# A ring of 24 heads for the cross attention's products, and gathers that read the table of slots itself, in a two-layer decoder kernel

## The chip, the cores and the metric

The kernel runs on one core of a Trainium2 chip. Its engines are TensorE (PE, with its weight loads shown as PEld), VectorE (DVE), ScalarE (ACT), GpSimd (POOL) and SyncE (SP, which only issues DMAs here); each has its own queue of instructions and runs it in order, and semaphores tie the queues together. The metric is the time of one execution on the device in microseconds, as the median of several runs.

## The reference, cut to what matters

The input is 64 sequences of 64 tokens with 256 channels, 4096 rows in all, that is 32 tiles of 128 rows. Six blocks follow one another, each with a layer norm ahead of it and a residual sum behind it: a linear attention, a recurrence over the context, a mixture of eight experts of which each token takes two, a banded attention, a cross attention and a gated feed-forward block with a small attention in it. The change lies in the stage that computes the last three. Its cross attention is unusual: for every token by itself, its 16 heads of the query look at the 16 heads of the context row at the same place.

```
Q = (q @ Wq.T + bq).reshape(bs, sl, H, HD)      # H = 16 heads of HD = 16
K = (k @ Wk.T + bk).reshape(bs, sl, H, HD)
V = (v @ Wv.T + bv).reshape(bs, sl, H, HD)
score = jnp.einsum('bshd,bsgd->bshg', Q, K)
weight = jax.nn.softmax(score, axis=-1)
attn = jnp.einsum('bshg,bsgd->bshd', weight, V).reshape(bs, sl, nf)
return attn @ Wo.T + bo
```

So a token has 16 x 16 scores, each a sum of 16 products, and then 256 outputs, each again a sum of 16 products. No weights are shared between tokens there, so this is not work for TensorE.

## The kernel before

The program has three stages: the linear attention (first, to about 1600 us), the recurrence with the experts (to about 2005 us), and `layer_one`, which computes the last three blocks and adds up the experts' outputs on its way. Only `layer_one` changes.

`layer_one` is a software pipeline over the 32 tiles. `FIRST` gives each piece of work a stage number (G = -2 gathers the experts' outputs, D and its helpers are the banded attention, En, E and Et the cross attention at 1, 2 and 3, F and Ft the attention of the last block, M and Md its feed-forward). `iterate` writes out one pass after another; in pass i a piece with stage number s works on tile i - s. Each engine has its own list of pieces, and the order of that list is the order of its instructions in every pass. Nothing is reordered by a scheduler.

POOL's list is: `power("F", 2)` (inverse roots for the last block's norm, written l_rsF), `products_av`, `power("D", 1)`, `power("E", 1)` (l_rsD and l_rsE), `products_qk`, `gather`. So in a pass POOL first makes the products of weights and values of tile t (16 instructions of 128x256, one for each head, L1740), then the products of queries and keys of tile t + 1 (16 more, L1733), then the gathers of a later tile.

Both kinds of product are written into one buffer, `prod`, of 16 heads (16 KB in each partition). DVE sums them up: four reductions of four heads each make the scores (`et_scores`, L2238), then `et_shift`, ACT's exponential (L2120) and `et_weights` (its last instruction is L2254, which counts the semaphore E_w up), and four more reductions make the attention's output (`et_values`, L2262, each of which counts E_att up). In DVE's list the four of a kind don't stand together: other pieces lie between them, and they come in the order of quarters 0, 2, 1, 3. `products_qk` of tile t waits until all four `et_values` of tile t - 1 have run, since it overwrites what they read:

```
wait_if(pool, S("E_att"), 4 * t)
...
for h in range(H):
    nc.gpsimd.tensor_tensor(out=prod[:, h], ...
```

`products_av` waits for E_w alone. `q`, the query, is one buffer, filled by ACT (L2016) once the products of the tile before are made; `kv`, the keys and values, is three buffers loaded by SP.

`gather` fetches the two experts' rows of each token with two indirect DMAs (L1752) which POOL itself describes. Their row numbers are first copied from the table `slots` (32 tiles x 2 numbers in each partition) into a small tile `of_tile` (L1747); a multiplication of constants into `ready` stands ahead of the copy and another behind it (L1746, L1750).

`fwo`, a weight of 256 x 256, has a buffer of its own; PE uses it once, at the very start of the stage, for a product with `fa` (woa).

Of the kernel before, what the change touches and what calls it, by code (L numbers as in the profile page):

```python
# [8 lines left out]
ALU = mybir.AluOpType  # L9
ACT = mybir.ActivationFunctionType  # L10

P = 128
SEQ = 64
SEQS = 64
D = 256
# [1527 lines left out]
def layer_one(nc, new_sem, x_sb, ident, slots, wts, outs, kvd, bias_rows, a):  # L1543
# [25 lines left out]
    AX = mybir.AxisListType.X  # L1569
    FIRST = dict(G=-2, Dn=-1, D=0, Dt=1, En=1, E=2, Et=3, F=4, Ft=5, M=7, Md=8)  # L1570
    with ExitStack() as ctx:
# [19 lines left out]
        fwqk, fwv, fwo = sb("fwqk", [P, DC, 4 * P]), sb("fwv", [P, DC, D]), sb("fwo", [P, DC, D])  # L1591
# [12 lines left out]
        of_tile, ready = sb("of_tile", [P, 2], mybir.dt.uint32), sb("ready", [P, 1])  # L1604
# [20 lines left out]
        prod = sb("prod", [P, H, H, HD])  # L1625
# [57 lines left out]
        def _(sp):  # L1683
# [3 lines left out]
            for tensor, name in ((fwo, "fwo"), (fa, "fa")):  # L1687
                sp.dma_start(tensor[:], a[name]).then_inc(S("wo_in"), 16)
# [22 lines left out]
        def _(pool):  # L1711
# [14 lines left out]
            def products_qk(t):  # L1726
                pool.wait_ge(S("E_q"), t + 1)
                pool.wait_ge(S(f"kv_in{t % 3}"), 16 * (t // 3 + 1))
                wait_if(pool, S("E_att"), 4 * t)
                qv = q[:].rearrange("p (h d) -> p h d", d=HD)  # L1730
                kk = kv[t % 3][:, 0, :].rearrange("p (g d) -> p g d", d=HD)
                for h in range(H):
                    nc.gpsimd.tensor_tensor(out=prod[:, h], in0=qv[:, h:h + 1, :].to_broadcast([P, H, HD]), in1=kk,  # L1733
                                            op=ALU.mult).then_inc(S("E_pqk"), 1)

            def products_av(t):
                pool.wait_ge(S("E_w"), t + 1)
                vv = kv[t % 3][:, 1, :].rearrange("p (d g) -> p d g", d=HD)
                for h in range(H):
                    nc.gpsimd.tensor_tensor(out=prod[:, h], in0=sco[:, h:h + 1, :].to_broadcast([P, HD, H]), in1=vv,  # L1740
                                            op=ALU.mult).then_inc(S("E_pav"), 1)

            def gather(t):
                wait_if(pool, S("G_ready"), 2 * t)
                wait_if(pool, S("G_x"), 2 * t)
                nc.gpsimd.tensor_tensor(out=ready[:], in0=neghalf[:, 0:1], in1=neghalf[:, 0:1], op=ALU.mult).then_inc(S("G_ready"), 1)  # L1746
                nc.gpsimd.tensor_copy(of_tile[:], slots[:, tile(t), :].rearrange("p t k -> p (t k)")).then_inc(S("G_at"), 1)  # L1747
                pool.wait_ge(S("G_ready"), 2 * t + 1)
                pool.wait_ge(S("G_at"), t + 1)
                nc.gpsimd.tensor_tensor(out=ready[:], in0=neghalf[:, 0:1], in1=neghalf[:, 0:1], op=ALU.mult).then_inc(S("G_ready"), 1)  # L1750
                for k in range(2):
                    nc.gpsimd.indirect_dma_start(got[k][:], None, outs[:, :],  # L1752
                                                 bass.IndirectOffsetOnAxis(ap=of_tile[:, k:k + 1], axis=0)).then_inc(S(f"G_in{k}"), 16)
# [394 lines left out]
        def _(dve):  # L2148
# [84 lines left out]
            def et_scores(k):  # L2233

                def piece(t):
                    wait_if(dve, S("E_pav"), H * t)
                    dve.wait_ge(S("E_pqk"), H * t + 4 * k + 4)
                    nc.vector.reduce_sum(sco[:, 4 * k:4 * k + 4, :], prod[:, 4 * k:4 * k + 4], axis=AX).then_inc(S("E_sc"), 1)  # L2238
                return piece
# [17 lines left out]
            def et_values(k):  # L2257

                def piece(t):
                    wait_if(dve, S("E_aTp"), t)  # L2260
                    dve.wait_ge(S("E_pav"), H * t + 4 * k + 4)
                    nc.vector.reduce_sum(att[:].rearrange("p (h d) -> p h d", d=HD)[:, 4 * k:4 * k + 4, :], prod[:, 4 * k:4 * k + 4],  # L2262
# [206 lines left out]
```

## Time and profile before

| | |
|---|---|
| three timed runs | 3121.44 us median, 3116.44 to 3129.29 |
| the profiled execution, from the first to the last instruction | 3137.3 us (its own time is not listed apart from this span) |
| the third stage in it | about 2005 to 3137 us |
| PE / DVE / ACT / POOL busy | 90% / 82% / 62% / 65% of the span |

The profiled execution is 15.9 us longer than the median. Starts in the rows are microseconds from its first instruction. A row of a timeline gives start, duration, engine, line, operation, what is written and read, the shapes, how many instructions are merged into the row, and in brackets how long the engine had been idle ahead of it and what ended that. A busy engine need not be one that others wait for; the list of waits tells this.

### The profile page before, as it was taken

What the parts mean: (1) busy time and instruction counts of PE and PEld (TensorE: products, weight loads), DVE (VectorE), ACT (ScalarE), POOL (GpSimd) and SP (SyncE); (2) the same over time, 40 slices, a digit from 0 to 9 for tenths busy, and PEclk for the clock granted to TensorE, in tenths of its full rate; (3) what the DMA queues carried; (4) which work ended last, traced back from release to release, by engine and by line L of the source; (5) the groups of instructions that cost most, each with busy time, mean ns of one, the idle gap of its engine ahead of it and who ended that gap; (6) DMA issues with size and microseconds to landing.
All of it is one profiled execution on the core that took longest, in us unless ns stands there. A gap on an engine that the chain in (4) does not pass through costs nothing. (4 is left out here: it accounts for less than half of the span.)

```text
span 3137.3 us, 68808 instructions
## 1 busy us (share of the span) xinstructions
PE 2826.3 (90%) x21864; PEld 2304.6 (73%) x21864; DVE 2581.5 (82%) x5745; ACT 1949.5 (62%) x4213; POOL 2038.0 (65%) x2535
## 2 busy tenths in 40 slices
PE   6999999999999999997786799657899999999978
PEld 3888888888888888886454577435777777777767
DVE  6888888888888888886597566478999999999973
ACT  5888877787877778785343333245565656565632
POOL 5886666666666666665487200178888888888870
PEclk8999999999999999998897899767999999999999
DMA  4564444444444444442422222300000000000000
GB/s 145 168 206 158 134 145 136 141 141 145 135 147 128 140 134 138 154 130 82 160 103 74 85 77 77 124 14 18 20 20 25 20 25 20 25 18 27 15 9 11
DMA packets 178643, 288.05 MB, mean 92 GB/s; under 512 B 42255, under 2 KB 103832, under 8 KB 177707
## 3 DMA queue, kind: packets, MB, share of 16 engines
q1 hardware_dynamic: 172206, 267.46, 25.8%
q0 software_dynamic: 6144, 16.79, 1.7%
q8 instruction: 171, 2.80, 0.3%
q14 instruction: 122, 1.00, 0.1%
HBM read 221.99 MB, written 53.78 MB: 88 GB/s over the span
## 5 line engine op out<-in xcount | busy, mean ns | idle before, releaser
L1740 POOL TENSOR_TENSOR l_prod<-l_sco,l_kv 128x256 f32<-128x256 f32 x512 | 380.0, 781 | 47.5 <-DVE l_sco L2254 47.5
L1733 POOL TENSOR_TENSOR l_prod<-l_q,l_kv 128x256 f32<-128x256 f32 x512 | 358.6, 740 | 62.1 <-DVE l_att L2262 62.1
L717 DVE SCALAR_TENSOR_TENSOR a_cq<-a_PQ,a_taps,a_cq 128x504 f32<-128x504 f32 (+2 forms) x384 | 281.7, 734 | 74.0 <-ACT a_cq L583 64.9
L717 DVE SCALAR_TENSOR_TENSOR a_ck<-a_PK,a_taps,a_ck 128x504 f32<-128x504 f32 (+2 forms) x384 | 280.6, 731 | 9.7 <-ACT a_ck L583 0.6
L341 POOL TENSOR_TENSOR a_tq<-a_cq,a_tq 128x512 f32<-128x512 f32 x128 | 165.5, 1293 | 131.3 <-ACT a_tq L589 131.2
L328 POOL TENSOR_TENSOR a_hrs<-a_hve,a_neghalf 128x8 f32<-128x8 f32 x128 | 209.4, 1636 | 25.9 <-DVE a_hve L734 25.4
L484 PE MATMUL a_Y<-a_wo,a_og_parts 128*128 128x256 f32 x1536 | 206.2, 284 | 4.2 <-POOL a_og_parts L335 4.2
L411 PEld LDWEIGHTS a_X<-a_wv,a_xb 128*128 128x128 f32 x1536 | 199.9, 188 | 12.1 <-issue 1.2
L411 PE MATMUL a_PQ<-a_x_hi,a_wqk 128*128 (+1 forms) x512 | 195.3, 422 | 12.0 <-issue 11.3
L341 POOL TENSOR_TENSOR a_tk<-a_ck,a_tk 128x512 f32<-128x512 f32 x128 | 163.3, 1276 | 64.1 <-ACT a_tk L589 64.1
L411 PE MATMUL a_X<-a_wv,a_xb 128*128 128x256 f32 x1536 | 204.2, 282 | 0.8 <-DMA a_xb<-a_x_lo 0.8
L484 PEld LDWEIGHTS a_Y<-a_wo,a_og_parts 128*128 128x128 f32 x1536 | 195.1, 192 | 5.5 <-issue 5.4
L602 ACT ACTIVATE a_hk<-a_PK,a_lncol 128x512 f32<-128x512 f32 x128 | 99.9, 781 | 154.5 <-PE a_PK L503 154.5
L596 ACT ACTIVATE a_nq<-a_TQ,a_hnb,a_hrs 128x128 f32<-128x128 f32 x512 | 191.6, 460 | 1.5 <-POOL a_hnb L331 1.0
L596 ACT ACTIVATE a_nk<-a_TK,a_hnb,a_hrs 128x128 f32<-128x128 f32 x512 | 191.1, 457 | 0.0
L411 PE MATMUL a_X<-a_x_hi,a_wg 128*128 (+1 forms) x512 | 184.3, 400 | 2.3 <-DVE a_og L742 2.3
L411 PE MATMUL a_PK<-a_x_hi,a_wqk 128*128 (+1 forms) x512 | 182.6, 397 | 0.0
L335 POOL TENSOR_TENSOR a_og_parts<-a_og,a_og_parts 128x512 fp32r<-128x512 f32 x128 | 166.1, 1298 | 19.9 <-ACT a_og_parts L609 19.9
L1712 POOL MEMSET l_cmask<- 128x512 bf16 x1 | 0.5, 524 | 255.4 <-POOLq L2354 255.4
L583 ACT ACTIVATE a_cq<-a_PQ,a_taps 128x512 f32<-128x512 f32 x128 | 99.8, 779 | 101.3 <-PE a_PQ L411 101.3
L771 DVE TENSOR_TENSOR_SCAN a_em<-a_dr,a_dm 128x256 f32<-128x256 f32 x128 | 159.7, 1247 | 0.0
L2262 DVE TENSOR_REDUCE l_att<-l_prod 128x64 f32<-128x1024 f32 x128 | 151.7, 1206 | 8.6 <-POOL l_prod L1740 8.3
(403 smaller groups left out, 8534.5 us busy)
## 6 DMA issues: line engine op xcount, KB each, us to landing
a_wqk<-qk_parts SPq DMA_DIRECT2D x112, 512.0 KB, 3.3
a_wv<-v_parts SPq DMA_DIRECT2D x56, 512.0 KB, 3.7
a_wg<-g_parts SPq DMA_DIRECT2D x112, 256.0 KB, 3.1
a_wo<-o_parts SPq DMA_DIRECT2D x112, 256.0 KB, 2.8
a_dr<-decays SPq DMA_DIRECT2D x256, 64.0 KB, 2.6
m_hs<-sorted_rows SPq DMA_DIRECT2D x72, 128.0 KB, 2.0
sorted_outs<-m_ys SPq DMA_DIRECT2D x72, 128.0 KB, 1.7
qk_parts<-a_wqk SPq DMA_DIRECT2D x16, 512.0 KB, 3.3
```

Source lines behind the costliest of these rows:

```text
L328: nc.gpsimd.tensor_tensor(out=hrs[q][:], in0=hve[q][:], in1=neghalf[:], op=ALU.pow).then_inc(s_hrstd, 1)
L335: nc.gpsimd.tensor_tensor(out=og_parts[q][:, 1, :], in0=og[q][:], in1=og_parts[q][:, 0, :].bitcast(F32), op=ALU.subtract).then_inc(og_lo, 1)
L341: nc.gpsimd.tensor_tensor(out=t[i][p][:], in0=c[i][p][:], in1=t[i][p][:], op=ALU.mult).then_inc(s_silu, 1)
L411: last = nc.tensor.matmul(out, lhs(i, k), rhs(j, k), start=at_pass == PASSES[0], stop=at_pass == PASSES[-1])
L484: last = nc.tensor.matmul(Y[:, j, :], og_parts[p][:, i, j * P:(j + 1) * P], wo[p][:, w, :], start=first and j % 2 == 0 and k == 0, stop=Tr ...
L596: nc.scalar.activation(nrm[i][q][:, j, :], TB[i][:, j, :], ACT.Identity, bias=hnb[q][:, k:k + 1], scale=hrs[q][:, k:k + 1]).then_inc(s_nor ...
L602: nc.scalar.activation(hat[i][q][:], PB[i][:], ACT.Identity, bias=lncol[:, 2 * i + 1:2 * i + 2], scale=lncol[:, 2 * i:2 * i + 1]).then_inc ...
L717: nc.vector.scalar_tensor_tensor(out=acc, in0=src, scalar=taps[p][:, tap + k:tap + k + 1], in1=acc, op0=ALU.mult, op1=ALU.add).then_inc(s_ ...
L771: nc.vector.tensor_tensor_scan(out=flat(em[q]), data0=flat(dr[q]), data1=flat(dm[q]), initial=0.0, op0=ALU.mult, op1=ALU.add).then_inc(s_e ...
L1733: nc.gpsimd.tensor_tensor(out=prod[:, h], in0=qv[:, h:h + 1, :].to_broadcast([P, H, HD]), in1=kk, op=ALU.mult).then_inc(S("E_pqk"), 1)
L1740: nc.gpsimd.tensor_tensor(out=prod[:, h], in0=sco[:, h:h + 1, :].to_broadcast([P, HD, H]), in1=vv, op=ALU.mult).then_inc(S("E_pav"), 1)
L2262: nc.vector.reduce_sum(att[:].rearrange("p (h d) -> p h d", d=HD)[:, 4 * k:4 * k + 4, :], prod[:, 4 * k:4 * k + 4], axis=AX).then_inc(S("E ...
```

## The change

`prod` becomes a ring of 24 heads. The products of tile t take 32 places in a row from place 32t on, modulo 24: the first 16 for queries and keys, the next 16 for weights and values. The first eight heads of `products_qk` of a tile then fall on places that nothing reads any more; heads 8 to 15 fall on the places of heads 0 to 7 of the tile before's weights and values, which the reductions of quarters 0 and 1 read. Since DVE's order is 0, 2, 1, 3, the wait now stands ahead of head 8 and asks for three reductions instead of four. The wait for the fourth moves to `products_av`. The reductions take their quarter at the same places.

The ring has 8 KB more in each partition. `fwo` loses its buffer (2 KB) and becomes a view of the ring's first two heads; it is loaded and used before the ring is. `gather` loses its copy, its two multiplications and their two semaphores, and the indirect DMA reads its row numbers from `slots`.

```diff
+    RING = 24
-        fwqk, fwv, fwo = sb("fwqk", [P, DC, 4 * P]), sb("fwv", [P, DC, D]), sb("fwo", [P, DC, D])
+        fwqk, fwv = sb("fwqk", [P, DC, 4 * P]), sb("fwv", [P, DC, D])
-        of_tile, ready = sb("of_tile", [P, 2], mybir.dt.uint32), sb("ready", [P, 1])
-        prod = sb("prod", [P, H, H, HD])
+        prod = sb("prod", [P, RING, H, HD])
+        fwo = prod[:, 0:2].rearrange("p h g d -> p h (g d)")
...
             def products_qk(t):
                 pool.wait_ge(S("E_q"), t + 1)
                 pool.wait_ge(S(f"kv_in{t % 3}"), 16 * (t // 3 + 1))
-                wait_if(pool, S("E_att"), 4 * t)
...
                 for h in range(H):
-                    nc.gpsimd.tensor_tensor(out=prod[:, h], in0=qv[:, h:h + 1, :].to_broadcast([P, H, HD]), in1=kk,
+                    if h == H // 2 and t:
+                        pool.wait_ge(S("E_att"), 4 * t - 1)
+                    nc.gpsimd.tensor_tensor(out=prod[:, (2 * H * t + h) % RING], in0=qv[:, h:h + 1, :].to_broadcast([P, H, HD]), in1=kk,
...
             def products_av(t):
                 pool.wait_ge(S("E_w"), t + 1)
+                wait_if(pool, S("E_att"), 4 * t)
...
-                    nc.gpsimd.tensor_tensor(out=prod[:, h], in0=sco[:, h:h + 1, :].to_broadcast([P, HD, H]), in1=vv,
+                    nc.gpsimd.tensor_tensor(out=prod[:, (2 * H * t + H + h) % RING], in0=sco[:, h:h + 1, :].to_broadcast([P, HD, H]), in1=vv,
...
             def gather(t):
-                wait_if(pool, S("G_ready"), 2 * t)
                 wait_if(pool, S("G_x"), 2 * t)
-                nc.gpsimd.tensor_tensor(out=ready[:], in0=neghalf[:, 0:1], in1=neghalf[:, 0:1], op=ALU.mult).then_inc(S("G_ready"), 1)
-                nc.gpsimd.tensor_copy(of_tile[:], slots[:, tile(t), :].rearrange("p t k -> p (t k)")).then_inc(S("G_at"), 1)
-                pool.wait_ge(S("G_ready"), 2 * t + 1)
-                pool.wait_ge(S("G_at"), t + 1)
-                nc.gpsimd.tensor_tensor(out=ready[:], in0=neghalf[:, 0:1], in1=neghalf[:, 0:1], op=ALU.mult).then_inc(S("G_ready"), 1)
                 for k in range(2):
                     nc.gpsimd.indirect_dma_start(got[k][:], None, outs[:, :],
-                                                 bass.IndirectOffsetOnAxis(ap=of_tile[:, k:k + 1], axis=0)).then_inc(S(f"G_in{k}"), 16)
+                                                 bass.IndirectOffsetOnAxis(ap=slots[:, t, k:k + 1], axis=0)).then_inc(S(f"G_in{k}"), 16)
...
             def et_scores(k):
...
-                    nc.vector.reduce_sum(sco[:, 4 * k:4 * k + 4, :], prod[:, 4 * k:4 * k + 4], axis=AX).then_inc(S("E_sc"), 1)
+                    at = (2 * H * t + 4 * k) % RING
+                    nc.vector.reduce_sum(sco[:, 4 * k:4 * k + 4, :], prod[:, at:at + 4], axis=AX).then_inc(S("E_sc"), 1)
```

`et_values` changes in the same way, with `at = (2 * H * t + H + 4 * k) % RING`.

The next fences show POOL's queue. In brackets stand the semaphores that an instruction waits for, under the names that their numbers had in the first stage: in the queue before, a_zset is E_w, a_zdec is E_att, a_zdecay is E_q, a_x_ld4 is the load of `kv`, a_xhi, a_zmm and a_nb_set are the statistics of D, E and F, and a_xrstd, a_xvar and a_xnorm are those of `gather`; in the changed queue, which has two fewer, a_zdecay is E_w, a_zdec is E_att, a_zmm is E_q, a_xT, a_xhi and a_zT are the statistics of D, E and F, and a_xvar is `gather`'s.

One pass in the middle of the stage on POOL, before: the products of weights and values, two powers, the products of queries and keys, the gather, a power.

```order
L1740 TENSOR_TENSOR l_prod<-l_sco,l_kv 128x256 [waits a_zset]
L1740 TENSOR_TENSOR l_prod<-l_sco,l_kv 128x256 x15
L1723 TENSOR_TENSOR l_rsD<-l_veD,l_neghalf 128x1 [waits a_xhi]
L1723 TENSOR_TENSOR l_rsE<-l_veE,l_neghalf 128x1 [waits a_zmm]
L1733 TENSOR_TENSOR l_prod<-l_q,l_kv 128x256 [waits a_zdec,a_x_ld4,a_zdecay]
L1733 TENSOR_TENSOR l_prod<-l_q,l_kv 128x256 x15
L1746 TENSOR_TENSOR l_ready<-l_neghalf 128x1 [waits a_xrstd,a_xvar]
L1747 COPY l_of_tile<-slots 128x2
L1750 TENSOR_TENSOR l_ready<-l_neghalf 128x1 [waits a_xnorm,a_xvar]
L1752 DMA l_got<-sorted_outs,l_of_tile 128x256 x2
L1723 TENSOR_TENSOR l_rsF<-l_veF,l_neghalf 128x2 [waits a_nb_set]
```

The same pass on POOL now:

```order
L1743 TENSOR_TENSOR l_prod<-l_sco,l_kv 128x256 [waits a_zdec,a_zdecay]
L1743 TENSOR_TENSOR l_prod<-l_sco,l_kv 128x256 x15
L1724 TENSOR_TENSOR l_rsD<-l_veD,l_neghalf 128x1 [waits a_xT]
L1724 TENSOR_TENSOR l_rsE<-l_veE,l_neghalf 128x1 [waits a_xhi]
L1735 TENSOR_TENSOR l_prod<-l_q,l_kv 128x256 [waits a_x_ld4,a_zmm]
L1735 TENSOR_TENSOR l_prod<-l_q,l_kv 128x256 x7
L1735 TENSOR_TENSOR l_prod<-l_q,l_kv 128x256 [waits a_zdec]
L1735 TENSOR_TENSOR l_prod<-l_q,l_kv 128x256 x7
L1749 DMA l_got<-sorted_outs,slots 128x256 [waits a_xvar]
L1749 DMA l_got<-sorted_outs,slots 128x256
L1724 TENSOR_TENSOR l_rsF<-l_veF,l_neghalf 128x2 [waits a_zT]
```

No instruction has changed its place in the queue; the wait for E_att has moved from the first product of queries and keys to the ninth, a second one stands at the first product of weights and values, and three small instructions ahead of the gathers are gone.

The start of the stage on POOL, before: the mask is made, then the first gather is set up.

```order
L1717 AFFINE_SELECT l_cmask<-l_cmask 64x512
L1746 TENSOR_TENSOR l_ready<-l_neghalf 128x1 [waits a_xstat]
L1747 COPY l_of_tile<-slots 128x2
L1750 TENSOR_TENSOR l_ready<-l_neghalf 128x1 [waits a_xnorm,a_xvar]
L1752 DMA l_got<-sorted_outs,l_of_tile 128x256 x2
```

The start of the stage on POOL now:

```order
L1718 AFFINE_SELECT l_cmask<-l_cmask 64x512
L1749 DMA l_got<-sorted_outs,slots 128x256 [waits a_xstat]
L1749 DMA l_got<-sorted_outs,slots 128x256
L1724 TENSOR_TENSOR l_rsD<-l_veD,l_neghalf 128x1 [waits a_xT]
L1749 DMA l_got<-sorted_outs,slots 128x256 [waits a_xvar]
```

The first gather stands right behind the mask (a_xstat counts the mask's instructions).

The end of the stage on POOL, before: the products of the last two tiles, with no power of D or E between them any more.

```order
L1740 TENSOR_TENSOR l_prod<-l_sco,l_kv 128x256 [waits a_zset]
L1740 TENSOR_TENSOR l_prod<-l_sco,l_kv 128x256 x15
L1733 TENSOR_TENSOR l_prod<-l_q,l_kv 128x256 [waits a_zdec,a_x_ld5,a_zdecay]
L1733 TENSOR_TENSOR l_prod<-l_q,l_kv 128x256 x15
L1723 TENSOR_TENSOR l_rsF<-l_veF,l_neghalf 128x2 [waits a_nb_set]
L1740 TENSOR_TENSOR l_prod<-l_sco,l_kv 128x256 [waits a_zset]
L1740 TENSOR_TENSOR l_prod<-l_sco,l_kv 128x256 x15
```

The end of the stage on POOL now:

```order
L1743 TENSOR_TENSOR l_prod<-l_sco,l_kv 128x256 [waits a_zdec,a_zdecay]
L1743 TENSOR_TENSOR l_prod<-l_sco,l_kv 128x256 x15
L1735 TENSOR_TENSOR l_prod<-l_q,l_kv 128x256 [waits a_x_ld5,a_zmm]
L1735 TENSOR_TENSOR l_prod<-l_q,l_kv 128x256 x7
L1735 TENSOR_TENSOR l_prod<-l_q,l_kv 128x256 [waits a_zdec]
L1735 TENSOR_TENSOR l_prod<-l_q,l_kv 128x256 x7
L1724 TENSOR_TENSOR l_rsF<-l_veF,l_neghalf 128x2 [waits a_zT]
```

Between the products of weights and values and the first eight of the next tile no wait for DVE is left.

## Rows read from the trace of the kernel before

**Rows 1.** The page: busy us, share of the span and instructions of each engine.
```profile
PE 2826.3 (90%) x21864; PEld 2304.6 (73%) x21864; DVE 2581.5 (82%) x5745; ACT 1949.5 (62%) x4213; POOL 2038.0 (65%) x2535
```

**Rows 2.** Windows, 24 whole passes: us, then busy of each engine, clock, DMA.
```profile
2189.21:2943.81 754.60, 686.75 (x5978) 552.71 (x5979) 718.57 (x1415) 449.33 (x1131) 656.52 (x960) 0.98 0.07 22
```

**Rows 3.** Waits, 2200 to 3000: engine, line, released by; total us, times, longest.
```profile
POOL l_prod L1733 <- DVE l_att L2262: 52.3, 25, 3.3
...
DVE l_att L2262 <- POOL l_prod L1740: 1.6, 1, 1.6
```

**Rows 4.** Timeline of POOL, one pass: start, us, line, instructions, idle ahead.
```profile
2488.50 12.00 POOL L1740 TENSOR_TENSOR l_prod<-l_sco,l_kv 128x256 f32<-128x256 f32 x16 [0.80 <-DVE l_sco L2254]
...
2500.96 0.54 POOL L1723 TENSOR_TENSOR l_rsE<-l_veE,l_neghalf 128x1 f32<-128x1 f32 x1
2503.44 11.08 POOL L1733 TENSOR_TENSOR l_prod<-l_q,l_kv 128x256 f32<-128x256 f32 x16 [1.95 <-DVE l_att L2262]
...
2515.60 1.06 POOL L1752 DMA_INDIRECT l_got<-sorted_outs,l_of_tile  x1 [0.46 <-issue]
...
2517.94 0.74 POOL L1723 TENSOR_TENSOR l_rsF<-l_veF,l_neghalf 128x2 f32<-128x2 f32 x1
2519.47 12.01 POOL L1740 TENSOR_TENSOR l_prod<-l_sco,l_kv 128x256 f32<-128x256 f32 x16 [0.80 <-DVE l_sco L2254]
```

**Rows 5.** Timeline of DVE in that pass, and one row of the next.
```profile
2499.63 2.33 DVE L2262 TENSOR_REDUCE l_att<-l_prod 128x64 f32<-128x1024 f32 x2
...
2504.44 0.44 DVE L2204 SCALAR_TENSOR_TENSOR l_hmD<-l_hmD,l_sink 128x16 f32<-128x16 f32 x1
...
2506.92 0.81 DVE L2279 TENSOR_TENSOR l_gm<-l_gmT,l_gm 16x128 fp32r<-16x128 f32 x1
...
2510.80 0.32 DVE L2209 TENSOR_SCALAR l_hmF<-l_hmF 128x16 f32<-128x16 f32 x1
...
2513.25 3.46 DVE L2238 TENSOR_REDUCE l_sco<-l_prod 128x64 f32<-128x1024 f32 x3
...
2542.25 0.79 DVE L2209 TENSOR_SCALAR l_hmF<-l_hmF 128x16 f32<-128x16 f32 x1
```

**Rows 6.** Timelines of POOL and DVE at the start of the stage.
```profile
2007.04 0.19 POOL L1746 TENSOR_TENSOR l_ready<-l_neghalf 128x1 f32<-128x1 f32 x1
...
2008.23 1.02 POOL L1752 DMA_INDIRECT l_got<-sorted_outs,l_of_tile  x1 [0.52 <-issue]
...
2015.18 0.48 DVE L2157 SCALAR_TENSOR_TENSOR x_sb<-l_got,wts,x_sb 128x256 f32<-128x256 f32 x1 [1.19 <-DMA l_got<-sorted_outs,l_of_tile]
...
2032.38 0.17 DVE L2204 SCALAR_TENSOR_TENSOR l_hmD<-l_hmD,l_sink 128x16 f32<-128x16 f32 x1
```

**Rows 7.** Timelines of POOL and DVE in the second and third pass with products.
```profile
2092.27 16.03 POOL L1733 TENSOR_TENSOR l_prod<-l_q,l_kv 128x256 f32<-128x256 f32 x16 [0.37 <-DVE l_att L2262]
...
2125.80 10.91 POOL L1733 TENSOR_TENSOR l_prod<-l_q,l_kv 128x256 f32<-128x256 f32 x16 [0.49 <-DVE l_att L2262]
...
2133.65 3.11 DVE L2209 TENSOR_SCALAR l_hmF<-l_hmF 128x16 f32<-128x16 f32 x1
```

**Rows 8.** Timelines of POOL and DVE in the last passes with products.
```profile
3004.88 11.02 POOL L1733 TENSOR_TENSOR l_prod<-l_q,l_kv 128x256 f32<-128x256 f32 x16 [2.02 <-DVE l_att L2262]
...
3019.85 10.98 POOL L1740 TENSOR_TENSOR l_prod<-l_sco,l_kv 128x256 f32<-128x256 f32 x16 [3.31 <-DVE l_sco L2254]
3036.24 11.02 POOL L1733 TENSOR_TENSOR l_prod<-l_q,l_kv 128x256 f32<-128x256 f32 x16 [5.41 <-DVE l_att L2262]
...
3015.99 1.22 DVE L2238 TENSOR_REDUCE l_sco<-l_prod 128x64 f32<-128x1024 f32 x1 [0.38 <-POOL l_prod L1733]
...
3027.94 3.17 DVE L2284 TENSOR_TENSOR l_x<-l_x2f,l_x 128x256 fp32r<-128x256 f32 x1
...
3044.65 2.35 DVE L2238 TENSOR_REDUCE l_sco<-l_prod 128x64 f32<-128x1024 f32 x2 [0.63 <-POOL l_prod L1733]
...
3047.36 1.22 DVE L2238 TENSOR_REDUCE l_sco<-l_prod 128x64 f32<-128x1024 f32 x1 [0.36 <-POOL l_prod L1733]
```

More of the change, by code:

```diff
@@ L1686, in _ @@
                 sp.dma_start(tensor[:], a[name]).then_inc(S("d_in"), 16)
-            for tensor, name in ((fwo, "fwo"), (fa, "fa")):
-                sp.dma_start(tensor[:], a[name]).then_inc(S("wo_in"), 16)
+            for tensor, name in ((fwo, "fwo"), (fa[:], "fa")):
+                sp.dma_start(tensor, a[name]).then_inc(S("wo_in"), 16)
             sp.dma_start(raw_in, a["win"]).then_inc(S("raw_in"), 16)
@@ L2261, in piece @@
                     dve.wait_ge(S("E_pav"), H * t + 4 * k + 4)
-                    nc.vector.reduce_sum(att[:].rearrange("p (h d) -> p h d", d=HD)[:, 4 * k:4 * k + 4, :], prod[:, 4 * k:4 * k + 4],
+                    at = (2 * H * t + H + 4 * k) % RING
+                    nc.vector.reduce_sum(att[:].rearrange("p (h d) -> p h d", d=HD)[:, 4 * k:4 * k + 4, :], prod[:, at:at + 4],
                                          axis=AX).then_inc(S("E_att"), 1)
```

## The prediction

> **What bounds the kernel now.** I read the page first [rows 1]: over the whole span DVE and PE are the busiest, POOL is at 65%. That mixes stages, so the next view is a window over 24 whole passes of the third stage, from the start of one tile's products of queries and keys to that of a tile 24 later [rows 2]: 754.60 us, 31.44 a pass. DVE is busy for 718.57 (95%), PE for 686.75 (91%), POOL for 656.52 (87%). The third view decides, the list of waits [rows 3]: POOL waited 52.3 us for DVE's reductions L2262 in 25 passes, about 2.1 each; this is the wait that the change takes away. The other way round DVE waited for POOL's products 1.6 us in 800. So in the middle of the stage POOL stands off the path: it is late only because DVE makes it late, and DVE doesn't notice.
>
> The timelines of one pass show the same in order [rows 4, 5]. POOL's products of weights and values run from 2488.50 to 2500.50 and the two powers to about 2501.5. Then it idles 1.95 us for the fourth reduction of quarters, makes the products of queries and keys to 2514.52, gathers, makes a power, and idles again (0.80) for DVE's softmax, which ends at 2519.4. DVE reads the last three quarters of those products from 2513.25 without a wait.
>
> **The change part by part.** The sum is made on the profiled execution, whose span is 15.9 us above the median; the difference is then taken off the median, 3121.44.
>
> *Middle of the stage, waits.* Now the products of queries and keys can start when the power l_rsE is done, at 2500.96 + 0.54, about 2501.5 [rows 4], 1.95 earlier. The ninth head is due 8 x 0.69 = 5.5 later, at 2507.0 (11.08 / 16 = 0.69 for one); the third reduction that it now waits for ended at 2499.63 + 2.33 = 2501.96 [rows 5]. So that wait costs nothing, and the fourth, at the products of weights and values, comes 16 us after its reduction (which ended just ahead of 2503.44). Behind it the gather saves its three small instructions: the first two starts in rows 6 are 2008.23 - 2007.04 = 1.19 apart, and with the idle time of 0.46 that still stands ahead of a DMA [rows 4] 0.7 is left. POOL then stands ready for the next products about 1.95 + 0.7 earlier, at 2516.1, and waits for the softmax at 2519.4 as before. Its start doesn't move, for DVE sets it. What is late next is DVE itself. Worth: 0.
>
> *Middle, the shared work of DVE and POOL.* Some small DVE instructions are longer beside POOL's products. L2204 takes 0.17 where POOL is idle [rows 6] and 0.44 one us into the products of queries and keys [rows 5]; 27 such rows read 0.43 to 0.45. It waits for the end of POOL's instruction: 1.00 / 0.69 = 1.45 instructions have gone, 0.38 us remain, 0.27 is seen. After the change the products start 1.95 earlier and L2204 comes 2.95 into them: 4.3 have gone, 0.5 us remains, so it should wait 0.34, or 0.07 more. The instructions behind it (L2279, L2209) keep their distances from it and so their waits. 27 x 0.07 = +1.9 us. Bounds: no wait, 27 x -0.27 = -7; a whole instruction's, 27 x (0.69 - 0.27) = +11. No other DVE instruction of two inputs in SBUF stands in the stretch that POOL newly fills (2501.5 to 2503.4) or newly leaves.
>
> *Start of the stage.* The first gather stands behind the mask and DVE waits 1.19 us for its rows [rows 6]. It is issued 0.7 earlier. Landing takes 5.9 us (2009.25 to 2015.18) beside the loads of all weights, so the rows may land when those let them: between 0 and -0.7; I take -0.4. Later gathers are needed a pass or more after they land.
>
> *First passes.* Tile 1's products wait 0.37 and tile 2's 0.49 [rows 7]. Here DVE does wait for POOL, so both come off the path: -0.85. In tile 2's pass L2209 took 3.11 us, to the moment when POOL's row of 16 products ended; that end also moves by 0.85. If it should not be held so this time, another 2 us go: from -0.85 to -3.
>
> *Last passes.* From 2944 on DVE has less to do. Tile 30's products wait 2.02, but DVE then waits for their end 0.38 only [rows 8]: -0.38. Tile 31's wait 5.41. They would start behind the products before, at 3019.85 + 10.98 - 0.38 = 3030.5, and end at 3041.5. DVE's last three score reductions then start when DVE is free, at 3044.65 - 0.63 - 0.38 = 3043.64, and take 3.46 as in rows 5, to 3047.10, where before they ended at 3047.36 + 1.22 = 3048.58: -1.48 with the 0.38 in it. So of 5.41 us only 1.1 is gained; DVE's other pieces cover the rest. From there one chain (softmax, last products, output, last tile's attention and feed-forward) leads to the end, so -1.5 stays. L2284 was held to the end of POOL's row here [rows 8], and now the next row follows without a pause; held on to its ninth head, at 3036, it would delay all this by 5 us and leave a loss of some 4. That is the upper bound, -1.5 the value, since the gap between the rows stays an instruction's.
>
> `fwo` as a view and the four extra places move nothing: the ring is first written when tile 0 has a query, and that comes behind `fwo`'s product in PE's queue. At nothing too are the reads from `slots`: the gather's own 1.06 and 0.95 us stay, and even doubled they would lie in POOL's idle 3.3 us.
>
> Sum: 0 + 1.9 - 0.4 - 0.85 - 1.5 = -0.85 us, so 3121.44 - 0.85 = 3120.6.
>
> **The rivals.** *DVE held to the end of POOL's row (slower).* Two DVE instructions were held not for one product but until the row of 16 was over: L2209 from 2133.65 to 2136.76, when POOL's row ended at 2136.71 [rows 7], and L2284 from 3027.94 to 3031.11, when POOL's row ended at 3030.83 [rows 8]. In the middle L2209 stands 7.36 into POOL's row and takes 0.32, in some passes 0.79 [rows 5]. Now it stands 9.3 into it with 1.8 to go. If every pass held it, 27 x (1.8 - 0.2) = +43 us, 3164; if L2204 were held until the new wait ahead of the ninth head, 5.5 - 2.95 - 0.27 = 2.3, 27 times, +62, 3183. It decides as soon as the hold happens in the repeating passes, since those are alike to 0.02 us. Against it: both cases lie in passes at the ends of the stage where pieces are still or already missing from DVE's list; in the middle L2279 comes between POOL's products 3 us ahead of L2209, before and after. Chance 0.08.
> The Trainium skill (SBUF — State Buffer, "Who interferes with whom") says that a DVE instruction with two SBUF inputs, and a GpSimd instruction that reads SBUF, take a shared pair of ports in turns, and that the loser is blocked for the whole of the other's instruction. By that rule a hold ends with one product, so the price would be at most the +11 above, about 3130; the rows with 3.11 and 3.17 go beyond it.
>
> *The passes even out (faster).* The pass in rows 4 lasts 30.97 (2488.50 to 2519.47), the mean is 31.44 [rows 2]; in some of the longer ones L2209 takes 0.79 [rows 5]. If POOL's new phase spared DVE that, 24 x 0.47 = -11.3 more, 3109. Against it: L2209's wait hangs on its distance to L2279, which doesn't change. Chance 0.12.
>
> *POOL sets the pace after all (faster).* Then 2.1 + 0.7 come off each of 27 passes: -76 us, 3046. DVE's 1.6 us of waits speak against it [rows 3]. Chance 0.03.
>
> *The change doesn't do what it says.* The products start where they did, held by E_q or the power instead. Against it: the row of the wait names the reduction as what came last, not E_q [rows 4], and l_rsE is done by 2501.5. Then the time is that of before, 3121, or up to 1 less for the gather. Chance 0.07.
>
> **How the numbers follow.** The forecast, DVE sets the pace, gets 0.70: 3120.6, with a range of its own from -7 - 0.7 - 3 - 1.5 = -12 to 11 - 0.85 + 4 = +14, 3109 to 3135, all within 0.5% (15.6 us, about what a measurement of this kernel can tell from no change); the three runs of before already spread over 13 us. Left out of the range are the held instruction (0.08), POOL's pace (0.03) and a few per cent of drift, so 3108 to 3135. Faster by over 0.5%: POOL's pace 0.03 and a sixth of the 0.12, where evening out and lower bounds add up past 15.6, and 0.05 for a gain that I don't see: 0.10. Slower: the held instruction 0.08 and 0.02 for the like: 0.10. Within 0.5%: 0.80.
>
> **What would show it.** Right, if POOL's wait for L2262 is gone in the list of waits and its wait for L2254 has grown from 0.8 to about 3.3 us a pass; if L2204 reads about 0.5 and L2209 0.3 or 0.8; if DVE stays at 95% in the middle; if tile 31's products start about 5.7 earlier and the last score reductions end 1.5 earlier. Wrong, if DVE's share falls or a pass is under 30.9 us (then POOL did set the pace), or if L2204, L2209 or L2284 read over 1 us in pass after pass.

## The result, and the profile after

The changed kernel takes 3288.98 us (median of four runs, 3253.97 to 3308.55); the kernel before, run beside it, took 3125.36. The ratio is 1.0474 (95% interval 1.0438 to 1.0509): 4.7% slower, outside the predicted range. This ratio leaves out the longest of the four, 3308.55, as a slow run; that is the one profiled, and the holds that its trace shows stand alike in a run that isn't slow (the one with one input, below). The profiled span is 3306.3 us, 169.0 above that of before. In the changed kernel L1735 are the products of queries and keys (before: L1733), L1743 those of weights and values (L1740), L2201 is the small DVE instruction that the prediction calls L2204, L2252 ends the softmax (L2254).

First the page: busy us, share of the span and instructions of each engine, then three groups (busy, mean ns of one, idle time ahead and its releaser).

```profile
PE 2849.2 (86%) x21864; PEld 2308.6 (70%) x21864; DVE 2740.3 (83%) x5745; ACT 1946.4 (59%) x4213; POOL 2010.1 (61%) x2439
...
L1743 POOL TENSOR_TENSOR l_prod<-l_sco,l_kv 128x256 f32<-128x256 f32 x512 | 380.7, 782 | 164.6 <-DVE l_sco L2252 164.6
L1735 POOL TENSOR_TENSOR l_prod<-l_q,l_kv 128x256 f32<-128x256 f32 x512 | 349.4, 722 | 0.0
L2201 DVE SCALAR_TENSOR_TENSOR l_hmD<-l_hmD,l_sink 128x16 f32<-128x16 f32 x32 | 213.7, 6677 | 1.1
```

The last of these groups in the kernel before:

```profile
L2204 DVE SCALAR_TENSOR_TENSOR l_hmD<-l_hmD,l_sink 128x16 f32<-128x16 f32 x32 | 13.6, 424 | 1.1
```

Beside [rows 1] DVE has 158.8 us more to do with the same 5745 instructions. One group of 32 has 200.1 us more: L2201, 16 elements in each partition, is busy for 6.7 us on average. Other small instructions of DVE have become shorter, which gives back the difference. POOL's wait ahead of the products of queries and keys, 52.3 us in [rows 3], is gone, as intended. The same 24 passes as in [rows 2], from tile 4's products to tile 28's (us, busy of PE, PEld, DVE, ACT and POOL, clock, DMA):

```profile
2200.80:3104.06 903.26, 713.42 (x5969) 560.45 (x5970) 848.67 (x1413) 445.87 (x1129) 638.08 (x889) 0.89 0.06 18
```

They take 903.26 us instead of 754.60. Of the 24, 21 last 38.52 on average and three 31.46; before, the mean was 31.44. So 21 x 7.08 = 148.7 us of the 169.0 lie here, and all in the 21. DVE is busy for 130.1 us of these (848.67 - 718.57); for the other 18.6 it waits longer than before. PE is busy 26.7 us longer at a mean granted clock of 0.89 (0.98 before), but for 79% of the time instead of 91%, and the waits below show it waiting for DVE. The rest, added up from the starts of the products, lies at the two ends of the stage: +18.7 in the first four passes, +8.8 behind tile 28's, and -7.2 ahead of the first products, whose start lies anywhere from 2054.53 to 2074.75 in the runs below.

What a long pass looks like: POOL and DVE, from 2412 on (start, us, instruction, idle ahead).

```profile
2424.63 0.53 POOL L1724 TENSOR_TENSOR l_rsE<-l_veE,l_neghalf 128x1 f32<-128x1 f32 x1
2425.14 10.89 POOL L1735 TENSOR_TENSOR l_prod<-l_q,l_kv 128x256 f32<-128x256 f32 x16
2436.20 1.04 POOL L1749 DMA_INDIRECT l_got<-sorted_outs,slots  x1 [0.17 <-issue]
...
2444.53 0.72 POOL L1724 TENSOR_TENSOR l_rsF<-l_veF,l_neghalf 128x2 f32<-128x2 f32 x1 [6.04 <-DVE l_veF L2173]
2450.58 12.02 POOL L1743 TENSOR_TENSOR l_prod<-l_sco,l_kv 128x256 f32<-128x256 f32 x16 [5.33 <-DVE l_sco L2252]
```

```profile
2425.75 1.20 DVE L2261 TENSOR_REDUCE l_att<-l_prod 128x64 f32<-128x1024 f32 x1
2426.88 1.20 DVE L2198 TENSOR_REDUCE l_hmD<-l_SS 128x16 f32<-128x1024 f32 x1
2428.11 7.95 DVE L2201 SCALAR_TENSOR_TENSOR l_hmD<-l_hmD,l_sink 128x16 f32<-128x16 f32 x1
2436.09 0.18 DVE L2204 TENSOR_TENSOR l_hmD<-l_sink,l_hmD 128x16 f32<-128x16 f32 x1
2436.38 1.23 DVE L2209 SCALAR_TENSOR_TENSOR l_exD<-l_SS,l_hmD 128x1024 f32<-128x1024 f32 x1
2437.63 0.28 DVE L2278 TENSOR_TENSOR l_gm<-l_gmT,l_gm 16x128 fp32r<-16x128 f32 x1
```

L2201 starts 2.97 us into POOL's row and ends at 2436.06; POOL's sixteenth product ends at 2436.03. Its successor of the same size takes 0.18. An instruction that stands like this until the row is over is called held from here on. In three of the 24 passes L2201 isn't held, in two of them at the same distance; here it stands 2620.72 - 2617.75 = 2.97 into the row (POOL, where the view ends within the row, then DVE):

```profile
2617.75 7.61 POOL L1735 TENSOR_TENSOR l_prod<-l_q,l_kv 128x256 f32<-128x256 f32 x11
```
```profile
2620.72 0.52 DVE L2201 SCALAR_TENSOR_TENSOR l_hmD<-l_hmD,l_sink 128x16 f32<-128x16 f32 x1
```

The other engines wait for what follows the held instruction. The list of waits from 2200 to 3105 (engine, released by; total us, times, longest):

```profile
PE l_SS L1794 <- DVE l_exD L2209: 148.2, 22, 8.8
ACT l_exD L2018 <- DVE l_exD L2209: 129.8, 22, 7.9
POOL l_rsF L1724 <- DVE l_veF L2173: 127.3, 21, 6.1
POOL l_prod L1743 <- DVE l_sco L2252: 126.7, 24, 5.8
```

The last and the first of them in the kernel before, from 2190 to 2944:

```profile
POOL l_prod L1740 <- DVE l_sco L2254: 26.0, 24, 1.8
...
PE l_SS L1797 <- DVE l_exD L2212: 1.7, 2, 1.1
```

### The profile page after: what moved, and what is told of

Read it like the earlier page. It is cut to its first block and busy times, and to the rows that moved or that the text cites. A ratio compares the mean times of both kernels' runs of the same rounds, so it can differ in the third digit from the quotient of the medians.

```text
span 3306.3 us, 68680 instructions
## 1 busy us (share of the span) xinstructions
PE 2849.2 (86%) x21864; PEld 2308.6 (70%) x21864; DVE 2740.3 (83%) x5745; ACT 1946.4 (59%) x4213; POOL 2010.1 (61%) x2439
## 5 line engine op out<-in xcount | busy, mean ns | idle before, releaser
L1743 POOL TENSOR_TENSOR l_prod<-l_sco,l_kv 128x256 f32<-128x256 f32 x512 | 380.7, 782 | 164.6 <-DVE l_sco L2252 164.6
L1735 POOL TENSOR_TENSOR l_prod<-l_q,l_kv 128x256 f32<-128x256 f32 x512 | 349.4, 722 | 0.0
L341 POOL TENSOR_TENSOR a_tq<-a_cq,a_tq 128x512 f32<-128x512 f32 x128 | 165.5, 1293 | 130.1 <-ACT a_tq L589 130.0
L2201 DVE SCALAR_TENSOR_TENSOR l_hmD<-l_hmD,l_sink 128x16 f32<-128x16 f32 x32 | 213.7, 6677 | 1.1
L1794 PE MATMUL l_SS<-l_cmask,l_identb 128*128 128x512 bf16 x64 | 29.9, 565 | 178.9 <-DVE l_exD L2209 178.9
L2261 DVE TENSOR_REDUCE l_att<-l_prod 128x64 f32<-128x1024 f32 x128 | 151.7, 1206 | 8.9 <-POOL l_prod L1743 8.6
```

Source lines behind the costliest of these rows:

```text
L341: nc.gpsimd.tensor_tensor(out=t[i][p][:], in0=c[i][p][:], in1=t[i][p][:], op=ALU.mult).then_inc(s_silu, 1)
L1735: nc.gpsimd.tensor_tensor(out=prod[:, (2 * H * t + h) % RING], in0=qv[:, h:h + 1, :].to_broadcast([P, H, HD]), in1=kk, op=ALU.mult).then_i ...
L1743: nc.gpsimd.tensor_tensor(out=prod[:, (2 * H * t + H + h) % RING], in0=sco[:, h:h + 1, :].to_broadcast([P, HD, H]), in1=vv, op=ALU.mult).t ...
L2201: nc.vector.scalar_tensor_tensor(out=hm[k][:, 1, :], in0=hm[k][:, 0, :], scalar=SC, in1=sink[:], op0=ALU.mult, op1=ALU.add).then_inc(S("D_ ...
```

## The experiments

Line numbers move by a few with each edit; the small instruction is the one that writes l_hmD from l_hmD and l_sink. The 24 passes are always those from tile 4's products of queries and keys to tile 28's. Each ratio is taken beside the kernel before in the same session (medians of 3131.51, 3130.85 and 3129.29 us in the three).

**What in the change does it?** The theory: the wait that was moved. Rivals: the ring's places, or the gathers.

*The wait back in its place*, ring and gathers as changed:

```diff
+                wait_if(pool, S("E_att"), 4 * t)
...
                 for h in range(H):
-                    if h == H // 2 and t:
-                        pool.wait_ge(S("E_att"), 4 * t - 1)
```

> The ring of 24 and the gathers from the table of slots stay; the wait for all four reductions stands ahead of the first product of queries and keys again. Theory (the 160 us are L2201 on DVE, held to the end of POOL's row of products because the row now starts 1.95 us earlier): the row starts 1.0 us ahead of that instruction as before, it takes 0.44 us in every pass, and the time is that of the kernel before, 3121 within 10. Rival (the place of the ring in SBUF, or reading row numbers from the table, costs the time): the time stays at 3250 to 3310.

Measured 3131.35 us, ratio 1.0004 (0.9990 to 1.0017). The small instruction stands 1.00 into the row again and takes 0.43 to 0.45 in all 24 passes:

```profile
2563.76 0.44 DVE L2200 SCALAR_TENSOR_TENSOR l_hmD<-l_hmD,l_sink 128x16 f32<-128x16 f32 x1
```

*The gathers alone* in the kernel before (the diff's `gather` and nothing else):

> The kernel before with only the gathers changed to read from the table of slots. Theory: no hold, POOL's products still start behind the fourth reduction; the first gather lands up to 0.7 us earlier, so 3118 to 3125. Rival (the gather's earlier descriptors or its reads from the table disturb DVE): slower by over 15 us.

Measured 3131.39, ratio 1.0003 (0.9983 to 1.0022). So neither the places in the ring nor the gathers cost anything that can be measured; the loss comes from the moved wait, by which POOL now starts its row right behind the row before.

**What is the hold?** *The row pushed against DVE* by a memory set of POOL (into a spare buffer, `gap`) ahead of it, a little longer in each pass:

```diff
+                if t >= 3:
+                    nc.gpsimd.memset(gap[:, 0:27 * (t - 2)], 0.0)
```

> The changed kernel with one memset of a spare buffer on POOL ahead of the first product of queries and keys of tiles 3 to 31, 27 elements long for tile 3 and 27 more for each further tile, so that the row starts between 0 and about 0.8 us later in steps of some 0.03 us. It is a map of one run: at which distance from the start of POOL's row is L2201 held. Theory A (what counts is the point within one POOL instruction of 0.68 us at which DVE asks): held and not held change over within the 0.8 us and come back after 0.68. Theory B (what counts is how far into the row DVE asks, beyond the first one or two products): held throughout, 2.1 to 3.0 us into the row. Theory C (chance, since at 2.97 us both occur): held and not held mixed at every distance.

One run, 3251.4 us. The distance into the row went from 2.88 down to 2.38 in the 24 passes, with three off the line (1.74, 3.00 and 3.16). Held were the seven passes from 2.84 to 2.71 without exception, and one at 3.00; the one at 2.88 was not, and below 2.71 both kinds mix, at the very same distance too. Two neighbours, 2.56 and 2.56 into their rows (which start at 2710.49 and 2749.34):

```profile
2713.05 8.35 DVE L2204 SCALAR_TENSOR_TENSOR l_hmD<-l_hmD,l_sink 128x16 f32<-128x16 f32 x1
...
2751.90 0.26 DVE L2204 SCALAR_TENSOR_TENSOR l_hmD<-l_hmD,l_sink 128x16 f32<-128x16 f32 x1
```

13 of 24 passes were held, always until the row ended. Where the instruction isn't held, it takes 0.22 to 0.60 (once 0.80), that is, at most about one product (0.68) more than the 0.17 with POOL idle. This is nearest to theory C: there are two outcomes, a wait of one product or of the whole rest of the row, and the distance in hundredths of a microsecond doesn't settle which.

*A pause of POOL ahead of each product of queries and keys*, by a wait for its own product before (the expectations call this a drained row):

```diff
                     if h == H // 2 and t:
                         pool.wait_ge(S("E_att"), 4 * t - 1)
+                    if h:
+                        pool.wait_ge(S("E_pqk"), H * t + h)
```

> The changed kernel, but each product of queries and keys waits for the one before it (on the semaphore that POOL counts itself), so that POOL's row has a gap behind each product. Theory (DVE is held because POOL's products follow each other without a gap): no hold over one product, L2201 under 0.8 us in every pass, row about 12 to 13 us instead of 10.9, and the time 3110 to 3130. Rival (something other than the gapless row makes L2201 slow): L2201 still takes 8 us and the time stays at 3250 to 3310.

Measured 3113.40, ratio 0.9936 (0.9913 to 0.9958): no hold in any row with pauses, and faster than both kernels. The instruction is at the same 2.97 and takes hardly longer than with POOL idle ([rows 6], 0.17); POOL's row has become 2 us longer:

```profile
2409.54 0.19 DVE L2203 SCALAR_TENSOR_TENSOR l_hmD<-l_hmD,l_sink 128x16 f32<-128x16 f32 x1
```
```profile
2406.57 12.95 POOL L1737 TENSOR_TENSOR l_prod<-l_q,l_kv 128x256 f32<-128x256 f32 x16
...
2423.86 12.01 POOL L1745 TENSOR_TENSOR l_prod<-l_sco,l_kv 128x256 f32<-128x256 f32 x16 [1.16 <-DVE l_sco L2254]
```

*One pause only*, ahead of the ninth product. The moved wait stands there too, but it is satisfied before POOL comes to it:

```diff
+                    if h == H // 2:
+                        pool.wait_ge(S("E_pqk"), H * t + h)
```

> The changed kernel, but ahead of the ninth product of queries and keys POOL waits also for its own eighth product, so that the row has one real gap in its middle. The disputed DVE instruction (D's shift, the two-input one) still starts about 2.97 us into the row, where seven products stand without a gap behind it to the ninth head at 5.5. Theory 'a gap ends the hold': it reads 2.5 to 2.9 us in most passes instead of 7.95, and the time is 3289 - 25 x 5.2 = about 3160. Rival 'who is held is held to the last product of the row': it still reads about 8 and the time is about 3289. Rival 'the hold needs the whole row of 16 ahead of it': it reads under 0.6 and the time is 3115 to 3131.

3168.78 in one run, beside 3130.85 for the kernel before. Held instructions now end at the pause, 5.5 us into the row; 15 of 24 passes hold one:

```profile
2392.93 0.51 DVE L2203 SCALAR_TENSOR_TENSOR l_hmD<-l_hmD,l_sink 128x16 f32<-128x16 f32 x1
2424.13 2.57 DVE L2203 SCALAR_TENSOR_TENSOR l_hmD<-l_hmD,l_sink 128x16 f32<-128x16 f32 x1
```

So a pause ends a hold. A wait for something that has long happened does not: in the changed kernel, with the moved wait alone at the ninth product, the instruction stood 7.95 us, past it.

*Three pauses*, ahead of the products 2, 5 and 8 (counted from 0):

```diff
+                    if h in (2, 5, 8):
+                        pool.wait_ge(S("E_pqk"), H * t + h)
```

> The changed kernel with an own wait of POOL ahead of the products 2, 5 and 8 of queries and keys alone, so three gaps instead of fifteen. The disputed instruction comes at 2.97 + 0.1 us, the sixth product stands at about 3.7. Theory 'a hold lasts to the next gap': it reads 0.5 to 0.8 in every pass, no pass is held, POOL's row is about 11.4 us long, and passes are about 30.5 us: 3112 to 3125, ratio 0.995 to 0.999. Rival 'one gap may be lost again': in a part of the passes it reads 2.7 (the second gap passed over), 3130 to 3170.

3118.97, ratio 0.9969 (0.9956 to 0.9983); the instruction reads 0.42 to 0.74 in all 24 passes, none is held, and a pass takes 30.80.

**Which instructions can be held?** *One input instead of two*: D's shift computed as F's is, which leaves out L2201 and its successor.

```diff
-                    if k == "D":
-                        nc.vector.scalar_tensor_tensor(out=hm[k][:, 1, :], in0=hm[k][:, 0, :], scalar=SC, in1=sink[:], op0=ALU.mult,
...
-                        nc.vector.tensor_tensor(out=hm[k][:, 2, :], in0=sink[:], in1=hm[k][:, 1, :], op=ALU.subtract).then_inc(S("D_shift"), 1)
...
+                    nc.vector.tensor_scalar(hm[k][:, 2, :], hm[k][:, 0, :], -SC, None, ALU.mult).then_inc(S(k + "_shift"), 1)
```

> The changed kernel, but D's shift is made as F's is, by one DVE instruction of one input (the maximum times a constant); the instruction with two inputs in SBUF, which was held, and its successor are left out. The value is the same but for rounding. Rows, ring and waits stay. Theory 'it is held because of its two inputs in SBUF': the new instruction at 2.97 reads 0.17 to 0.6 and the time is 3289 - 25 x 7.0 = about 3115. Rival 'any DVE instruction from SBUF to SBUF that starts in the row may lose so': it reads 7.9 in most passes and the time is 3280 to 3290. Rival 'the hold moves to the next such instruction' (the difference of the two parts of the modulation, about 2 us behind it): that one reads up to 5.5 and the time is about 3220 to 3250.

3293.99, ratio 1.0516 (1.0490 to 1.0543): the first rival, a little above its range. An instruction with one input from SBUF is held just the same, in 21 of 24 passes:

```profile
2427.80 7.94 DVE L2200 TENSOR_SCALAR l_hmD<-l_hmD 128x16 f32<-128x16 f32 x1
```

*No shift at all*: DVE subtracts the maximum from the scores, which it reads from PSUM, and ACT's exponential takes the factor. L2201, L2204 and L2206 fall away.

```diff
...
+                    nc.vector.tensor_tensor(out=ex[k][:], in0=ss, in1=hm[k][:, 0, :].unsqueeze(2).to_broadcast([P, H, SEQ]),
+                                            op=ALU.subtract).then_inc(S(k + "_arg"), 1)
...
-                    nc.scalar.activation(ex[k][:], ex[k][:], ACT.Exp).then_inc(S(k + "_exp"), 1)
+                    nc.scalar.activation(ex[k][:], ex[k][:], ACT.Exp, scale=SC).then_inc(S(k + "_exp"), 1)
```

> The changed kernel without the disputed instruction and its two kindred (the shifts of D and F): DVE subtracts the maximum from the scores directly (scores from PSUM), and ACT's exponential takes the factor. Rows of products, ring and waits stay as in the changed kernel, with no gaps. Theory 'the loss sits in that one instruction, and the ring by itself is worth what the passes without a hold show' (31.05 us a pass in the changed kernel and 30.51 in the run with one gap, beside 31.44 before): two dependent instructions with 0.5 + 0.6 us fall away from each pass for D and 0.3 for F: about 30 us a pass, 3090 to 3115, a ratio of 0.985 to 0.995. Rival 'the hold moves to the next instruction from SBUF to SBUF in the same row' (the difference of the modulation's two parts, then some 4 us into the row): it reads up to 7 us in a part of the passes, 3150 to 3300.

3241.19, ratio 1.0369 (1.0339 to 1.0399): the rival again. The subtraction from PSUM takes 1.22 at 3.04 into the row, but the next instruction with both inputs in SBUF, 4.3 us into it in most passes, is held in 19 of 24 passes (35.77 us each; the other five take 29.92):

```profile
2747.90 0.64 DVE L2270 TENSOR_TENSOR l_gm<-l_gmT,l_gm 16x128 fp32r<-16x128 f32 x1
2778.05 6.75 DVE L2270 TENSOR_TENSOR l_gm<-l_gmT,l_gm 16x128 fp32r<-16x128 f32 x1
```

The prediction cited the Trainium skill (SBUF — State Buffer, "Who interferes with whom"), by which the loser waits for one instruction. The same section names tensor_scalar among the operations that can take the shared ports, and says that tensor_reduce never contends; L2200 above agrees with the first, and L2261, a reduction of products in SBUF that takes 1.20 us within POOL's row, with the second. On the length the measurement decides: 7.95 us is 7.95 / (10.89 / 16) = 11.7 products, not one.

**Is the ring worth anything?** *The pauses in the kernel before*, its waits and its one buffer kept:

```diff
+                    if h:
+                        pool.wait_ge(S("E_pqk"), H * t + h)
                     nc.gpsimd.tensor_tensor(out=prod[:, h], ...
```

> The kernel before, with only the own wait of POOL ahead of each product of queries and keys (no ring, no new gather). It tells what the 0.64% of the drained ring was. Theory 'the gain is the drain's, the ring gives nothing': DVE's small instructions lose their 0.27 and 0.6 us waits in each pass, ratio 0.993 to 0.996, about 3111. Rival 'the drain needs the slack that the ring gave POOL': its row is 1.9 us longer, POOL had 0.80 + 0.46 us of idle time behind it, so it ends about 0.7 us late for the softmax or the reductions in each pass: 3121 - 20 + 19 = within 0.2% of before, 3115 to 3128.

3190.10, ratio 1.0186 (1.0172 to 1.0201), worse than either expectation. POOL still waits 2 to 3 us for DVE, its row is 1.8 us longer (12.88), the products of weights and values follow without idle time, and now others wait for POOL (waits from 2300 to 2940):

```profile
POOL l_prod L1735 <- DVE l_att L2264: 50.2, 19, 3.2
...
ACT l_nmF L2000 <- POOL l_rsF L1723: 31.5, 20, 2.0
...
DVE l_sco L2240 <- POOL l_prod L1735: 11.1, 23, 0.9
```

A pass takes 33.14; two of the 24, of 39.10 and 39.28 us, also have a hold like those of the next run, the others take 32.58. So here the pauses pay only with the slack that the moved wait and the shorter gather give POOL (1.16 us left in the run with pauses, above).

*The shifts left out of the kernel before*, with the same edit:

> The kernel before, with only the shifts left out as in the run without the shifts (no ring, old gather). It parts the ring's share of a gain from the shifts' share. Theory 'the ring is worth 0.4 to 0.9 us a pass once nothing is held': this kernel gains 27 x (0.44 + 0.3 + 0.3) = about 28 us, ratio 0.990 to 0.994, and the ring with the same edit is 10 to 20 us better. Rival 'the ring is worth nothing in any case': both are alike within 0.2%.

3121.69, ratio 0.9982 (0.9968 to 0.9996), a smaller gain than the theory's. In two of its passes, without any ring, a DVE instruction of `d_rope`, a piece of the banded attention, is held through the other row of POOL (weights and values; 2200.35 to 2211.31):

```profile
2201.99 9.61 DVE L2190 TENSOR_TENSOR l_qkt<-l_qr,l_rt 128x256 f32<-128x256 f32 x1
```
```profile
2200.35 10.96 POOL L1740 TENSOR_TENSOR l_prod<-l_sco,l_kv 128x256 f32<-128x256 f32 x16
```

The two passes with it last 37.84 and 37.34, the other 22 take 30.50 on average, 0.94 less than the 31.44 of before. So two holds take back 14.2 us of what the edit gains, and the ring itself is not what makes a hold possible. POOL's row of 16 is 10.96 us here, where it is 12.0 beside a DVE that isn't held.

*Ring, pauses and no shifts together:*

> As the run without the shifts, and POOL also waits for its own product ahead of each product of queries and keys. Theory: what was lost to holds and single waits in that row is gone already, the drain adds 1.9 us to POOL's row, which POOL's slack covers (26.3 us of waits for the softmax in 21 passes of the drained ring, 1.25 each) only as long as DVE's pass is not shorter than POOL's 12.0 + 12.95 + 4.5 = 29.5 us and the order of their waits; 3095 to 3112. Rival: POOL becomes the bound as in the old kernel with the drain: 3120 or more.

3098.34, ratio 0.9906 (0.9888 to 0.9925): the best version, 0.9% faster than the kernel before and 5.8% than the changed one. None of the 24 passes has a hold, and one takes 30.10. That is 23.35 us ahead of the kernel just above; by the traces 14.2 of them are its two holds, and 24 x (30.50 - 30.10) = 9.6 is what the ring, the gather and the pauses add in passes without a hold. What the ring gives alone, with neither holds nor pauses, no run shows.

*Pauses in both rows*, the shifts kept:

> The changed kernel with an own wait of POOL ahead of each product in both rows (queries and keys as in the run with drained rows, and weights and values too). Theory 'what is gained there comes from DVE's instructions that no longer wait for POOL': the second row is about 0.125 x 15 = 1.9 us longer, POOL still has slack (it waited 51.5 us for the softmax in the run with one drained row, about 1.6 a pass), DVE's instructions beside the second row get shorter by some tenths, but POOL's pass grows to just about DVE's: within 0.3% of the kernel with one drained row, 3104 to 3122. Rival 'POOL becomes the bound': 0.3 to 0.8 us more a pass, 3122 to 3137.

3141.76, ratio 1.0028 (1.0011 to 1.0045): slower than with one row of pauses, 3113.40. POOL's second row grows from 12.0 to 13.2 us, DVE starts to wait for products (10.1 us in 18 waits from 2300 to 2940), and a pass takes 31.52. That POOL comes to bound it, the rival, fits; it ended a little above that rival's range.

## Why the prediction was wrong

- *Middle, waits: right.* POOL's idle time for the reductions is 0.0 instead of 52.3 us, and its wait for the softmax grew instead. In the three passes without a hold that costs nothing: 31.46 beside 31.44.
- *Middle, the shared work of DVE and POOL: the step that failed.* The term for L2204 was 27 x 0.07 = 1.9 us with +11 as its upper bound. The place was right: 2.95 into the row was forecast, 2.96 to 3.00 measured in 20 of the 21 held passes. The size was not: a wait of 0.34 was forecast, and the instruction took 7.94 to 7.96 in those 20 (9.01 in the 21st, at 1.92), which makes a held pass 7.08 us longer. The term and its bound took it that an instruction waits for one product of POOL at most. The rows with 3.11 and 3.17 [rows 7, 8] already showed the other outcome; the prediction saw it and kept it out of the range, as a rival with a small chance. Its own sign of being wrong, L2204 over 1 us in pass after pass, is what came.
- *The rival "DVE held to the end of POOL's row"* was the right mechanism at the right instruction, with a chance of 0.08 and a price of 2.3 us a pass instead of 7.1. Both the price and the argument behind the chance were wrong. The price took the satisfied wait ahead of the ninth product as a pause; the run with one real pause there is what gave 2.57. The argument against it, that the two holds lay in passes at the ends of the stage where DVE's list is incomplete, was a coincidence taken for a cause: with the list complete L2201 is held in the middle, and so, for 9.6 and 9.2 us, is an instruction of `d_rope` in the kernel before with its shifts left out or pauses put in. Why the middle of the kernel before has no hold stays as open as what decides between the two outcomes. That a hold repeats, since the passes are alike, came true 21 times of 24.
- *L2279 and L2209 keep their distances and so their waits: wrong, at little cost.* Behind a hold they run with POOL's row over: 0.28 and 0.17 instead of 0.81 and 0.32 to 0.79. With L2201's successor (0.18 instead of 0.65) that takes at least 1.1 us off the 7.95 - 0.44 = 7.51 of the hold. A held pass is still 7.08 longer, since DVE then waits for the scores of F that PE makes late (21.8 us from 2200 to 3105; 1.6 in the 24 passes before).
- *Start, gathers, `fwo`: right as far as can be measured.* DVE's wait for the first rows fell from 1.19 us to nothing, yet the gathers alone give 1.0003.
- *First passes:* whether the 0.85 was gained isn't shown, since holds bury it; all four rows from tile 1's products to tile 4's have one, of 9.55, 9.39, 8.18 and 9.01 us.
- *Last passes: right in direction, too small.* Tile 31's products start 31.36 + 2.02 - 27.72 = 5.66 us earlier (5.7 forecast). From the fourth reduction ahead of tile 30's products to the end it is 3137.3 - 3003.51 = 133.79 us before and 3306.3 - 3179.39 = 126.91 after, -6.9 instead of -1.5. Of the other 5.4, 5.1 fit the two holds of L2284 at the end, 3.17 [rows 8] and a second of 3.49, which read 0.68 and 0.86 now; the upper bound of +4 had the first longer. That is luck: one such hold is there again in the run with the gathers alone (2.95), three in the one with the wait back (up to 5.45).

## What to carry to other kernels

A row of GpSimd instructions that follow each other without a pause can hold a small VectorE instruction until it is over. Giving an off-path engine its idle time back moves its rows against the other engines' instructions, and here that was enough. Where a trace shows even one or two such holds, price the whole rest of the row in every repeating pass, and don't take it for unlikely because it has been rare so far. Pauses of 0.13 us (a wait for the engine's own last result) in the row capped the price here, where that engine had slack for them.

## What the runs showed of the hardware

- An instruction of 16 elements a partition on DVE stood for up to 9.6 us beside POOL's products; in the changed kernel it ends 0.03 to 0.04 us behind the row's last product, in the run with one pause at that pause. Such a pause cost (12.95 - 11.06) / 15 = 0.13 us of POOL's time, 11.06 being the row of a pass without a hold.
- A wait that was already satisfied when POOL arrived did not end a hold (7.95 us from 2.97 on, past the ninth product at 5.5).
- POOL's row is shorter while DVE is held: 10.96 instead of 12.0 us for the products of weights and values (the run with the shifts left out of the kernel before), 10.88 to 10.91 instead of 10.98 to 11.07 for those of queries and keys (the 24 passes of the changed kernel). So in passes without a hold POOL loses time beside DVE too.
- Held were instructions with two inputs in SBUF and some of a single input (7.94 in the run with one input; L2209 in [rows 7]); the reductions and the subtraction from PSUM that stand in the same rows read 1.20 to 1.23 throughout.
- What decides between a wait of one product and of the whole row stays open. At one and the same distance (2.56 us) one pass was held and another not. Other distances were never held: in the kernel before L2204 at 1.00 and L2279 at 3.47 took 0.43 to 0.45 and 0.79 to 0.81 in all 24 passes. No run here tells what differs.
